# Seven split down products a slot, an input normalised a slot early, and routing tables in PSUM: one change to the front of a six-layer kernel

## The chip, the core and the metric

The kernel runs on one core of one Trainium2 chip. Its time is device microseconds of one execution. The engines of the core work in parallel, each through its own list of instructions in order, and they meet at semaphores: TensorE (PE, with its weight loads PEld), VectorE (DVE), ScalarE (ACT), GpSimd (POOL) and SyncE (SP), which here only starts transfers. Products are written by TensorE to PSUM, which has eight banks here: G, V, U, C, Y, Z and S0, S1.

## The reference, cut to what matters

Sixteen batches of 512 rows by 128 columns go through six layers, all in float32:

```
x = x + 0.5 * moe(layernorm(x))        # L0_ffn
x = x + gated_attention(layernorm(x))  # L0_attn
x = x + 0.5 * moe(layernorm(x))        # L0_ffn again, same weights
x = x + 0.5 * mlp(layernorm(x))        # L1_ffn, relu
x = x + softmax_attention(layernorm(x))  # L1_attn
x = x + 0.5 * mlp(layernorm(x))

moe(x): scores = sigmoid(x @ gate.T); the two best of 16, divided by (their sum + 1e-20) -> comb
        g = silu(x @ We_gate[e]); u = x @ We_up[e]          # 16 experts, 64 wide
        y = sum_e comb[e] * ((g * u) @ We_down[e])
        shared = (silu(x @ Ws_gate) * (x @ Ws_up)) @ Ws_down  # 128 wide
        return y + shared
```

The first four layers are the kernel's front (`build_front`), the last two its back. The change touches the front alone, and within it the MoE and its routing.

## The kernel before, in words

A batch lies on the chip as 128 partitions by T = 4 tiles by 128. The front works in slots. A slot computes one MoE layer of one batch, the main work, and beside it one other layer, the side work, of another batch. The loop `turns` (8) times `NM` (4) slots has side work ATT, MLP, ATT, MLP (`SIDE`); one slot without side work stands ahead of the loop and one behind it, 34 slots in all. The main input of a slot is prepared in the slot before it. The inputs are numbered q as the slots are; with odd q the input is a fresh batch in `xin`, loaded from memory; with even q it is the result `xw` of a side layer.

A slot has NT = 9 passes n = 0 to 8. Pass n takes 128 columns of the hidden width: n = 0 is the shared expert, n = 1 to 8 are two routed experts each. In each pass TensorE forms the gate product in G and the up product in U, each as three products of 512 columns of split operands (high times high, low times high, high times low; lines 903 to 905), and for n above 0 spreads the routing weights into C (line 955). ScalarE takes `s` = silu(G) (line 581). VectorE takes `su` = U*s (line 738) and `h` = C*su (line 749; for n = 0 `h` = U*s).

The down product of each `h` is made in one of two ways. In bank Y four products of 128x128 with float32 `h` as weights (`down`, line 910) give the result in its final layout. In bank V the result comes transposed: ScalarE rounds `h` to `hh` (`high`, line 565), GpSimd forms the rest `hl` = h - hh (`low`, line 432), and TensorE makes three products of 512 columns (lines 919, 921, 922), of which the first needs `hh` and the others stand behind a wait for `hl`. Before the change the passes 2 to 6 (V0 = 2, NV = 5) go to V and the passes 0, 1, 7 and 8 to Y; at the end ScalarE copies V to `vs` and TensorE adds its transposes to Y. I write V(k) or Y(k) for the down product of pass k. TensorE issues the down product of pass n-2 in pass n, except that Y(0) and Y(1) are issued a pass earlier, in passes 1 and 2.

The input's preparation runs through four engines: statistics on VectorE (`main_stats`), 1/sqrt and two 128x512 operations on GpSimd (`main_normalise`, result `z`), transposes of `z` into bank Z on TensorE (line 888), the rounding `xh` on ScalarE and its rest `xl` on VectorE (line 663), router products into Z (lines 895, 897), then the logits `lg`, an exponential on ScalarE and some 20 small VectorE operations on 128x64 tables (`routing_scores` to `routing_weights`, lines 675 to 724), and at last the transposes of `comb` into Z in the next slot's pass 0. The table `PREPARE` says in which pass each step stands in the lists.

The side work begins with statistics `mv_s` on VectorE, a scale and offset (`off_s`) on GpSimd, the normalised `zs` on ScalarE in pass 1, transposes into S0 by TensorE in pass 2 (line 963), `xhs` on ScalarE, `xls` on VectorE, and products of `xhs` and `xls`: those of the ATT slot at line 987, those of the MLP slot at lines 903 to 905 with output S.

No scheduler decides the order. Each engine's list is written out by hand in its own function `slot`, and GpSimd's in its loop; what stands earlier in a list is waited for by all that stands later.

Of the kernel before, what the change touches and what calls it, by code (L numbers as in the profile page):

```python
# [30 lines left out]
E = 16  # L31
# [3 lines left out]
V0, NV = 2, 5  # L35
# [22 lines left out]
class Chain:  # L58
# [114 lines left out]
def build_front(nc, weights, early, x_dram, mid_dram, ident_dram, staged_dram, tail_dram, turns):  # L173
    w = weights
    with ExitStack() as ctx:
# [34 lines left out]
        en = sb("en", [P, T, E])  # L210
        sc = sb("sc", [P, T, E])
        hit = sb("hit", [P, T, E])
        first = sb("first", [P, T, E])
        second = sb("second", [P, T, E])
        rest = sb("rest", [P, T, E])
        share = sb("share", [P, T, E])
        m1 = sb("m1", [P, T, 1])
        m2 = sb("m2", [P, T, 1])
        r1 = sb("r1", [P, T, 1])
        den = sb("den", [P, T, 1])  # L220
        comb = sb("comb", [P, T, E])
        comb2 = sb("comb2", [P, T, P])
        combh = sb("combh", [P, T, E], F32R)
# [33 lines left out]
        S = [ps(f"S{k}", [P, T, P]) for k in range(2)]  # L257

# [72 lines left out]
        block = ctx.enter_context(nc.Block())  # L331

# [66 lines left out]
        def _(pool):  # L399
# [20 lines left out]
            def main_normalise(q, i):  # L420
                rsqrt(rstd[:, :, 0], vpe, mv, mv_ready, mv_ready.at(i, q + 1), rstd_ready)
# [7 lines left out]
            def low(m, n, i):  # L429

                pool.wait_ge(hh_ready.sem, hh_ready.at(i, NV * m + n - V0 + 1))
                nc.gpsimd.tensor_tensor(hl[n % 3][:], h[n % 3][:], hh[n % 3][:],  # L432
                                        ALU.subtract).then_inc(hl_ready.sem, 1)
# [14 lines left out]
            own.step(nc.gpsimd.tensor_tensor(w["wdl"][:], w["wd"][:, V0:V0 + NV], w["wdh"][:], ALU.subtract))  # L448
            own.settle()
            main_normalise(0, 0)  # L450
            lows(-1, 0, range(V0, V0 + NV))
# [6 lines left out]
            for i in range(turns):  # L458
                for m in range(NM):
                    side_start(m, i, m)  # L460
                    if SIDE[m] == MLP:
                        main_normalise(m + 1, i)
                        lows(m, i, (2,))
                        side_bias(m, i, m)
                        lows(m, i, (3, 4, 5, 6))
                    else:
                        a = nth(m)
                        main_normalise(m + 1, i)
                        lows(m, i, (2,))
                        side_bias(m, i, m)  # L470
                        lows(m, i, (3,))
# [22 lines left out]
            lows(0, turns, (2, 3))  # L494
# [15 lines left out]
            lows(0, turns, (4, 5, 6))  # L510

        @block.scalar
        def _(act):
# [9 lines left out]
            def scores(q, i):  # L523
                act.wait_ge(lg_ready.sem, lg_ready.at(i, q + 1))
                nc.scalar.activation(en[:], lg[:], ACT.Exp, scale=-1.0).then_inc(score_ready.sem, 1)
# [37 lines left out]
            def high(m, n, i):  # L563
                act.wait_ge(h_ready.sem, h_ready.at(i, TE * m + n))
# [1443 lines left out]
```

## Time and profile before

| | |
|---|---|
| median of three runs | 1959.18 us (1956.84 to 1959.87) |
| the profiled execution | 1958.95 us, its span 1957.2 us |
| first slot's first gate product | 36.70 us |
| the last slot, from its first gate product to its last down product | 1094.86 to 1132.02 us |
| PE busy, share of the span | 1860.5 us, 95% |
| DVE, ACT, POOL busy | 1553.3, 1272.9, 886.6 us |
| granted TensorE clock, mean | 0.986 |

A busy share of TensorE counts modelled ends of products that overlap, so the distance between the starts of two products is the better measure of what one costs. A slot lasts about 32 us: ATT slots 32.3 us, MLP slots 31.8 us, measured between the first U products of one slot and of the next.

### The profile page before, as it was taken

Reading aid. Unit: us, or ns where it says so; the run is one execution under the profiler, and the core shown is the slowest. Engines: PE = TensorE matmul, PEld = TensorE weight load, DVE = VectorE, ACT = ScalarE, POOL = GpSimd, SP = SyncE. Lnnn points to the kernel's source line nnn. Section 1 sums busy time; section 2 is a strip of 40 time slices with the busy share of each in tenths; the row PEclk is TensorE's granted clock in tenths of the full one; section 3 lists DMA queues with packets and bytes.
Section 4 is the critical chain, followed back from the end, with each engine's and each line's share of the span. In section 5 each row is a group of like instructions: output and inputs, shape, how many; then the busy total and the mean of one; then the engine's idle time right before and its main releaser. Section 6 shows DMA issues by size and latency. Waiting matters only on the chain. (4 is left out here: it accounts for less than half of the span.)

```text
span 1957.2 us, 33103 instructions
## 1 busy us (share of the span) xinstructions
PE 1860.5 (95%) x11626; PEld 1258.0 (64%) x11626; DVE 1553.3 (79%) x3824; ACT 1272.9 (65%) x2383; POOL 886.6 (45%) x939
## 2 busy tenths in 40 slices
PE   2999999999999999999999889999999999999996
PEld 2788888888888888888888634444444444444433
DVE  5777777787777877787778479999999999999991
ACT  3555555555555565555555438888888888888884
POOL 2645654565556554655466323333333333333311
PEclk9999999999999999999999969999999999999998
DMA  3000000000000000000100032222222222222210
GB/s 134 7 12 1 12 12 12 1 12 12 12 1 12 12 12 12 1 12 12 37 2 6 6 96 90 90 91 91 91 91 91 89 88 88 88 92 84 92 39 12
DMA packets 49989, 85.74 MB, mean 44 GB/s; under 512 B 6752, under 2 KB 11104, under 8 KB 49760
## 3 DMA queue, kind: packets, MB, share of 16 engines
q1 hardware_dynamic: 47920, 81.85, 13.2%
q8 instruction: 93, 1.52, 0.3%
q10 hardware_dynamic: 1904, 1.78, 0.3%
q14 instruction: 72, 0.59, 0.1%
HBM read 49.26 MB, written 34.87 MB: 43 GB/s over the span
## 5 line engine op out<-in xcount | busy, mean ns | idle before, releaser
L1599 DVE TENSOR_REDUCE b_nm<-b_MX 128x1 f32<-128x512 f32 x1024 | 648.9, 683 | 46.5 <-PE b_MX L1707 30.0
L1491 ACT ACTIVATE b_pr<-b_ST 128x512 f32<-128x512 f32 x1024 | 550.1, 603 | 101.4 <-PE b_ST L1695 97.1
L581 ACT ACTIVATE s<-G 128x512 f32<-128x512 f32 x306 | 182.7, 597 | 184.5 <-PE G L905 158.5
L432 POOL TENSOR_TENSOR hl<-h,hh 128x512 fp32r<-128x512 f32 x170 | 219.3, 1290 | 180.6 <-ACT hh L565 180.6
L738 DVE TENSOR_TENSOR su<-U,s 128x512 f32<-128x512 f32 x272 | 187.2, 688 | 130.5 <-PE U L905 72.5
L1707 PE MATMUL b_MX<-b_kt,b_qt 32*128 32x512 f32 x768 | 240.8, 505 | 2.2 <-DVE b_nm L1599 1.8
L1695 PE MATMUL b_ST<-b_qt,b_kt 32*128 32x512 f32 x768 | 213.7, 494 | 6.1 <-ACT b_pr L1491 6.1
L1695 PEld LDWEIGHTS b_ST<-b_qt,b_kt 32*128 32x128 f32 x768 | 83.4, 181 | 204.0 <-ACT b_pr L1491 137.0
L749 DVE TENSOR_TENSOR h<-C,su 128x512 f32<-128x512 f32 x272 | 188.1, 691 | 9.3
L910 PE MATMUL Y<-w_wd,h 128*128 128x128 f32 x1088 | 145.3, 276 | 6.7 <-DVE h L749 6.7
L910 PEld LDWEIGHTS Y<-w_wd,h 128*128 128x128 f32 x1088 | 137.7, 192 | 16.8 <-DVE h L749 10.5
L1722 PE MATMUL b_PV<-b_pr,e_va 128*32 128x512 f32 x1024 | 139.0, 615 | 0.0
L903 PE MATMUL G<-xh,w_wgh 128*128 128x512 f32 x306 | 136.0, 444 | 0.7 <-ACT s L581 0.7
L1722 PE MATMUL b_PV<-b_pr,b_va 128*32 128x512 f32 x1024 | 136.4, 605 | 0.0
L903 PE MATMUL U<-xh,w_wuh 128*128 128x512 f32 x306 | 126.0, 412 | 1.1 <-DVE h L738 0.7
L905 PE MATMUL G<-xl,w_wgh 128*128 128x512 f32 x306 | 121.4, 397 | 0.0
L904 PE MATMUL G<-xh,w_wgl 128*128 128x512 f32 x306 | 121.2, 396 | 0.0
L905 PE MATMUL U<-xl,w_wuh 128*128 128x512 f32 x306 | 120.8, 395 | 0.0
L904 PE MATMUL U<-xh,w_wul 128*128 128x512 f32 x306 | 119.7, 391 | 0.0
L955 PE MATMUL C<-cT,w_pairs 128*128 128x512 f32 x272 | 107.7, 396 | 0.0
L1707 PEld LDWEIGHTS b_MX<-b_kt,b_qt 32*128 32x128 f32 x768 | 96.0, 185 | 15.8 <-DVE b_nm L1599 11.5
L565 ACT ACTIVATE hh<-h 128x512 fp32r<-128x512 f32 x170 | 105.9, 623 | 0.0
(308 smaller groups left out, 4075.4 us busy)
## 6 DMA issues: line engine op xcount, KB each, us to landing
b_kt<-staging SPq DMA_DIRECT2D x48, 256.0 KB, 3.0
b_qt<-staging SPq DMA_DIRECT2D x48, 256.0 KB, 3.4
staging<-e_khi SPq DMA_DIRECT2D x32, 256.0 KB, 2.9
staging<-e_qhi SPq DMA_DIRECT2D x32, 256.0 KB, 3.1
xin<-in_x SPq DMA_DIRECT2D x17, 256.0 KB, 2.8
mid<-xo SPq DMA_DIRECT2D x16, 256.0 KB, 2.0
staging<-e_klo SPq DMA_DIRECT2D x16, 256.0 KB, 3.0
staging<-e_qlo SPq DMA_DIRECT2D x16, 256.0 KB, 3.0
```

The lines of the kernel that those rows point to most:

```text
L432: nc.gpsimd.tensor_tensor(hl[n % 3][:], h[n % 3][:], hh[n % 3][:], ALU.subtract).then_inc(hl_ready.sem, 1)
L738: nc.vector.tensor_tensor(out[:], U[:], sbuf_s[n % 2][:], ALU.mult).then_inc(up_used.sem, 1)
L749: nc.vector.tensor_tensor(h[n % 3][:], C[:], su[n % 2][:], ALU.mult).then_inc(h_ready.sem, 1)
L903: pe.matmul(flat(bank), wh, flat(high), start=True, stop=False)
L904: pe.matmul(flat(bank), wl, flat(high), start=False, stop=False)
L905: return pe.matmul(flat(bank), wh, flat(low), start=False, stop=True)
L910: mm = pe.matmul(bank[:, t], hid[:, t], wd, start=(first and t == 0), stop=True, skip_group_check=True)
L1491: nc.scalar.activation(pr[k % 2][:, j], bank[:].rearrange("p a b -> p (a b)"), ACT.Exp, scale=SM_SCALE).then_inc(used["st"].sem, 1)
L1599: nc.vector.tensor_reduce(nm[g % 2][:, c:c + 1], bank[:].rearrange("p a b -> p (a b)"), AX.X, ALU.max).then_inc(used["mx"].sem, 1)
L1695: pe.matmul(flat(bank_of(B, "st", 0, u)), kt_[g][rows_of(j), k % T], flat(qt[g])[rows_of(j)], start=True, stop=True).then_inc(made["st"].s ...
L1707: pe.matmul(flat(bank_of(B, "mx", rel, u)), qt[g][rows_of(j), u // HG % T], flat(kt_[g])[rows_of(j)], start=True, stop=True).then_inc(made ...
L1722: mm = pe.matmul(flat(PV)[rows_of(j)], values_of(va[B.parity], kt, g, j), pr[k % 2][:, j], start=(k % (PAIR * T) == 0), stop=((k + 1) % (P ...
```

## The change

It does five things to the front.

1. `V0` goes and NV is 7: the passes 0 to 6 go to V, and 7 and 8 to Y. V(k) is issued in pass k+2 for all k, so nothing of the down products stands in pass 1. ScalarE and GpSimd have two more pieces (`high`, `low`) a slot, for passes 0 and 1. In pass 2 ScalarE's rounding of h(1) stands behind `side_high`; GpSimd's `low` of 0 and 1 stand behind the side's scale and offset.
2. The inputs with odd q, which the MLP slots use, have their statistics (pass 5) and `main_normalise` a slot earlier: in an MLP slot GpSimd now normalises the input m+1 behind `low` 0 and 1, and the input m+2 behind `low` 4. The first slot does this too.
3. In an ATT slot the transposes of `z` stand in pass 1 (before 3) and the router products in pass 2 (before 4); the exponential stays in pass 5. ScalarE's `xh` now stands before `zs` there.
4. The tables `en`, `sc`, `hit`, `rest`, `second`, `share` and `comb` lie in bank Z in place of SBUF. `combh` is gone: the rounding is written straight into `comb2`, one small operation less a slot. The two best scores share a tile, and their sum is a reduction.
5. `routed` of pass n at n of 3 and above always waits for `hl` of pass n-3.

The GpSimd list at the start of an MLP slot, before (`off_s`: the side's offset; `vpe`, `rstd`, `z`: `main_normalise`; `hl`: one `low` each; `xb`: side bias):

```order
L418 TENSOR_SCALAR off_s<-off_s 128x4
L405 TENSOR_TENSOR vpe<-mv,w_eps 128x4
L407 TENSOR_TENSOR rstd<-vpe,w_minus_half 128x4
L424 TENSOR_TENSOR z<-xw,mv 128x512
L427 TENSOR_TENSOR z<-z,rstd 128x512
L432 TENSOR_TENSOR hl<-h,hh 128x512
L445 TENSOR_TENSOR xb<-xw,w_b2h 128x512
L432 TENSOR_TENSOR hl<-h,hh 128x512 x4
```

And the same place now:

```order
L418 TENSOR_SCALAR off_s<-off_s 128x4
L435 TENSOR_TENSOR hl<-h,hh 128x512 x2
L405 TENSOR_TENSOR vpe<-mv,w_eps 128x4
L407 TENSOR_TENSOR rstd<-vpe,w_minus_half 128x4
L427 TENSOR_TENSOR z<-xw,mv 128x512
L430 TENSOR_TENSOR z<-z,rstd 128x512
L435 TENSOR_TENSOR hl<-h,hh 128x512
L448 TENSOR_TENSOR xb<-xw,w_b2h 128x512
L435 TENSOR_TENSOR hl<-h,hh 128x512 x2
L405 TENSOR_TENSOR vpe<-mv,w_eps 128x4
L407 TENSOR_TENSOR rstd<-vpe,w_minus_half 128x4
L427 TENSOR_TENSOR z<-xin,mv 128x512
```

Two `hl` moved ahead of the first normalisation, and a second normalisation came in between the `hl` of passes 4 and 5.

TensorE's list in an MLP slot, end of pass 2, before (C: routing weights; S: transposes of `zs`; Y: down product of pass 1):

```order
L955 MATMUL C<-cT,w_pairs 128x512
L963 MATMUL S<-w_ident,zs 128x128 x4
L910 MATMUL Y<-w_wd,h 128x128 x4
L903 MATMUL G<-xh,w_wgh 128x512
L904 MATMUL G<-xh,w_wgl 128x512
```

And now:

```order
L968 MATMUL C<-cT,w_pairs 128x512
L934 MATMUL V<-hh,w_wdh 128x512
L936 MATMUL V<-hh,w_wdl 128x512
L937 MATMUL V<-hl,w_wdh 128x512
L976 MATMUL S<-w_ident,zs 128x128 x4
L919 MATMUL G<-xh,w_wgh 128x512
```

The down product of pass 0 came here, in V and ahead of the transposes; Y(1) left.

TensorE's list in an ATT slot, end of pass 1, before:

```order
L955 MATMUL C<-cT,w_pairs 128x512
L910 MATMUL Y<-w_wd,h 128x128 x4
L903 MATMUL G<-xh,w_wgh 128x512
L904 MATMUL G<-xh,w_wgl 128x512
L905 MATMUL G<-xl,w_wgh 128x512
```

And now:

```order
L968 MATMUL C<-cT,w_pairs 128x512
L904 MATMUL Z<-w_ident,z 128x128 x4
L919 MATMUL G<-xh,w_wgh 128x512
L920 MATMUL G<-xh,w_wgl 128x512
L921 MATMUL G<-xl,w_wgh 128x512
```

The transposes of the next input took the place of Y(0).

The diff, cut to its core:

```diff
-V0, NV = 2, 5
+NV = 7
+INPUT_STATS = 5
 PREPARE = {
-    MLP: {"statistics": 1, "transpose": 4, "low": 4, "logits": 5, "scores": 6, "best": 6, "next": 7, "weights": 8},
-    ATT: {"statistics": 1, "transpose": 3, "low": 3, "logits": 4, "scores": 5, "best": 6, "next": 7, "weights": 8},
+    MLP: {"statistics": 1, "transpose": 4, "low": 4, "logits": 5, "exponential": 6, "scores": 6, "best": 6, "next": 7, "weights": 8},
+    ATT: {"transpose": 1, "low": 1, "logits": 2, "exponential": 5, "scores": 5, "best": 6, "next": 7, "weights": 8},
 }
...
+        en, sc, hit, rest, second, share = (Z[:, :, k * E:(k + 1) * E] for k in range(2, 8))
+        comb, total_score = en, second[:, :, 0:1]
...
             main_normalise(0, 0)
-            lows(-1, 0, range(V0, V0 + NV))
+            lows(-1, 0, range(5))
+            main_normalise(1, 0)
+            lows(-1, 0, range(5, NV))
...
                     if SIDE[m] == MLP:
+                        lows(m, i, (0, 1))
                         main_normalise(m + 1, i)
                         lows(m, i, (2,))
                         side_bias(m, i, m)
-                        lows(m, i, (3, 4, 5, 6))
+                        lows(m, i, (3, 4))
+                        if has_input(m + 2, i):
+                            main_normalise(m + 2, i)
+                        lows(m, i, (5, 6))
                     else:
                         a = nth(m)
-                        main_normalise(m + 1, i)
-                        lows(m, i, (2,))
+                        lows(m, i, (0, 1))
                         side_bias(m, i, m)
-                        lows(m, i, (3,))
+                        lows(m, i, (2, 3))
...
-                    if V0 < n <= V0 + NV:
+                    if 1 <= n <= NV and n != 2:
                         high(m, n - 1, i)
                     if n == 1 and side:
+                        if side == ATT:
+                            main_high(m + 1, i)
                         side_normalise(m, i, m)
                     if n == 2 and side:
                         side_high(i, m)
+                    if n == 2:
+                        high(m, n - 1, i)
...
-                step(nc.vector.tensor_copy(combh[:], comb[:]))
-                own.settle()
-                step(nc.vector.tensor_copy(comb2[:, :, 0:E], combh[:]))
+                step(nc.vector.tensor_copy(comb2[:, :, 0:E].bitcast(F32R), comb))
...
-                if n >= V0 + 3:
-                    dve.wait_ge(hl_ready.sem, hl_ready.at(i, NV * m + n - V0 - 2))
-                elif n >= 3:
-                    dve.wait_ge(down_done.sem, down_done.at(i, g0 + n - 2))
+                if n >= 3:
+                    dve.wait_ge(hl_ready.sem, hl_ready.at(i, NV * m + n - 2))
...
+                        if n == INPUT_STATS and side != ATT and has_input(m + 2, i):
+                            main_stats(m + 2, i)
...
-                    if n == 2 and side == MLP:
-                        side_transposes(i, m)
...
-                    if 1 <= n <= V0:
-                        moe_down(m, n - 1, i)
-                    if n >= V0 + 2:
+                    if n >= 2:
                         moe_down(m, n - 2, i)
                     if n == NT - 1:
                         moe_down(m, NT - 2, i)
+                    if n == 2 and side:
+                        side_transposes(i, m)
```

## Rows read from the trace of the kernel before

**Rows 1.** windows, a stretch of the front: engines busy, granted clock, DMA share, GB/s
```profile
480.00:600.00 120.00, 118.28 (x688) 100.98 (x687) 90.58 (x263) 65.53 (x118) 63.91 (x73) 1.00 0.03 10
```

**Rows 2.** timeline, TensorE (start, us, engine, line ...), MLP slot from 551.82
```profile
551.82 0.48 PE L903 MATMUL U<-xh,w_wuh 128*128 128x512 f32 x1
...
559.04 1.06 PE L910 MATMUL Y<-w_wd,h 128*128 128x128 f32 x8
559.85 0.48 PE L903 MATMUL G<-xh,w_wgh 128*128 128x512 f32 x1
...
565.22 0.40 PE L921 MATMUL V<-hh,w_wdl 128*128 128x512 f32 x1
...
565.68 0.40 PE L903 MATMUL G<-xh,w_wgh 128*128 128x512 f32 x1
```

**Rows 3.** timeline, GpSimd, the same MLP slot
```profile
556.51 0.23 POOL L418 TENSOR_SCALAR off_s<-off_s 128x4 f32<-128x4 f32 x1
558.54 0.20 POOL L405 TENSOR_TENSOR vpe<-mv,w_eps 128x4 f32<-128x4 f32 x1 [1.79 <-DVE mv L642]
...
562.06 1.30 POOL L432 TENSOR_TENSOR hl<-h,hh 128x512 fp32r<-128x512 f32 x1
```

**Rows 4.** timeline, ScalarE, the same MLP slot
```profile
559.24 0.60 ACT L543 ACTIVATE xhs<-S 128x512 fp32r<-128x512 f32 x1 [0.33 <-PE S L963]
```

**Rows 5.** timeline, TensorE, ATT slot from 519.49
```profile
519.49 0.48 PE L903 MATMUL U<-xh,w_wuh 128*128 128x512 f32 x1
...
528.66 0.45 PE L987 MATMUL S<-w_wkvuh,xhs 128*128 128x384 f32 x1
...
529.82 0.60 PE L888 MATMUL Z<-w_ident,z 128*128 128x128 f32 x4
530.17 0.48 PE L903 MATMUL G<-xh,w_wgh 128*128 128x512 f32 x1
...
532.92 0.18 PE L895 MATMUL Z<-w_router,xh 128*128 128x32 f32 x1
...
533.73 0.47 PE L919 MATMUL V<-hh,w_wdh 128*128 128x512 f32 x1
...
550.91 1.16 PE L910 MATMUL Y<-w_wd,h 128*128 128x128 f32 x8 [0.42 <-DVE h L749]
```

**Rows 6.** waits of weight loads from 120 to 960: total, times, longest, us
```profile
PEld S L1010 <- issue: 5.4, 13, 0.4
PEld S L987 <- DVE xls L762: 5.3, 13, 0.4
```

**Rows 7.** timeline, GpSimd, the ATT slot from 519.49
```profile
534.99 1.80 POOL L474 TENSOR_TENSOR kc<-kvu,w_sin_t 128x512 f32<-128x512 f32 x1 [1.35 <-ACT kvu L600]
...
546.38 1.30 POOL L432 TENSOR_TENSOR hl<-h,hh 128x512 fp32r<-128x512 f32 x1
548.03 1.28 POOL L490 TENSOR_TENSOR og<-on,uw 128x512 f32<-128x512 f32 x1 [0.36 <-ACT on L529]
```

**Rows 8.** timeline, VectorE, ATT and then MLP slot: one line, two lengths
```profile
548.30 1.09 DVE L710 TENSOR_TENSOR second<-hit,r 128x64 f32<-128x64 f32 x1
...
570.15 0.23 DVE L667 TENSOR_TENSOR lg<-Z,lb 128x64 f32<-128x64 f32 x1 [1.40 <-ACT lb L521]
...
579.08 0.22 DVE L710 TENSOR_TENSOR second<-hit,r 128x64 f32<-128x64 f32 x1
```

**Rows 9.** timeline, GpSimd, the first slot
```profile
50.11 0.20 POOL L405 TENSOR_TENSOR vpe<-mv,w_eps 128x4 f32<-128x4 f32 x1 [16.23 <-DVE mv L642]
...
53.61 2.55 POOL L432 TENSOR_TENSOR hl<-h,hh 128x512 fp32r<-128x512 f32 x2
```

**Rows 10.** timeline, TensorE, the first slot
```profile
55.65 0.39 PE L903 MATMUL G<-xh,w_wgh 128*128 128x512 f32 x1
```

**Rows 11.** timeline, ScalarE, the last slot
```profile
1107.21 0.63 ACT L565 ACTIVATE hh<-h 128x512 fp32r<-128x512 f32 x1
```

**Rows 12.** timeline, TensorE, the last slot
```profile
1115.69 1.11 PE L1024 MATMUL Z<-w_ident,e_xn 128*128 128x128 f32 x4 [7.96 <-POOL e_xn L509]
```

More of the change, by code:

```diff
@@ L209, in build_front @@
         lg = sb("lg", [P, T, E])
-        en = sb("en", [P, T, E])
-        sc = sb("sc", [P, T, E])
-        hit = sb("hit", [P, T, E])
         first = sb("first", [P, T, E])
[L214 to L218, printed above, removed]
+        best = sb("best", [P, T, 2])
+        m1, m2 = best[:, :, 0:1], best[:, :, 1:2]
         r1 = sb("r1", [P, T, 1])
         den = sb("den", [P, T, 1])
-        comb = sb("comb", [P, T, E])
         comb2 = sb("comb2", [P, T, P])
-        combh = sb("combh", [P, T, E], F32R)
         cT = [sb(f"cT{p}", [P, T, P], F32R) for p in range(2)]
@@ L509, in _ @@
             nc.gpsimd.tensor_tensor(early.xn[:], early.xn[:], w["lnsb"][:], ALU.add).then_inc(early.xn_ready.sem, 1)
-            lows(0, turns, (4, 5, 6))
+            lows(0, turns, range(4, NV))
         @block.scalar
@@ L593, in slot @@
                         side_high(i, m)
-                    if prepare and n == steps["logits"] + 1:
+                    if n == 2:
+                        high(m, n - 1, i)
+                    if prepare and n == steps["exponential"]:
                         scores(m + 1, i)
@@ L608, in slot @@
                     if prepare:
-                        if n == steps["transpose"]:
+                        if n == steps["transpose"] and side != ATT:
                             main_high(m + 1, i)
@@ L687, in routing_best @@
                 own.settle()
-                step(nc.vector.tensor_reduce(r1[:], hit[:], AX.X, ALU.max))
+                step(nc.vector.tensor_reduce(r1[:], hit, AX.X, ALU.max))
                 own.settle()
-                step(nc.vector.tensor_tensor(first[:], hit[:], wide(r1), ALU.is_equal))
+                step(nc.vector.tensor_tensor(first[:], hit, wide(r1[:]), ALU.is_equal))
                 own.settle()
-                step(nc.vector.scalar_tensor_tensor(out=rest[:], in0=first[:], scalar=-2.0, in1=sc[:],
+                step(nc.vector.scalar_tensor_tensor(out=rest, in0=first[:], scalar=-2.0, in1=sc,
@@ L693, in routing_best @@
                                                     op0=ALU.mult, op1=ALU.add))
                 own.settle()
-                step(nc.vector.tensor_reduce(m2[:], rest[:], AX.X, ALU.max))
+                step(nc.vector.tensor_reduce(m2, rest, AX.X, ALU.max))
             def routing_next(q, i):
                 own.settle()
-                step(nc.vector.tensor_tensor(hit[:], rest[:], wide(m2), ALU.is_equal))
-                step(nc.vector.tensor_tensor(den[:], m1[:], m2[:], ALU.add))
+                step(nc.vector.tensor_tensor(hit, rest, wide(m2), ALU.is_equal))
@@ L707, in routing_next @@
                 own.settle(1)
-                step(nc.vector.reciprocal(den[:], den[:]))
-                own.settle(1)
-                step(nc.vector.tensor_tensor(second[:], hit[:], wide(r1), ALU.is_equal))
-                own.settle(1)
-                step(nc.vector.tensor_tensor(share[:], sc[:], wide(den), ALU.mult))
+                step(nc.vector.reciprocal(den[:], total_score))
+                own.settle()
+                step(nc.vector.tensor_tensor(second, hit, wide(r1[:]), ALU.is_equal))
@@ L714, in routing_weights @@
+                step(nc.vector.tensor_tensor(share, sc, wide(den[:]), ALU.mult))
             def routing_weights(q, i):
                 own.settle(1)
-                step(nc.vector.tensor_tensor(first[:], first[:], second[:], ALU.add))
+                step(nc.vector.tensor_tensor(first[:], second, first[:], ALU.add))
                 own.settle()
-                step(nc.vector.tensor_tensor(comb[:], first[:], share[:], ALU.mult))
+                step(nc.vector.tensor_tensor(comb, share, first[:], ALU.mult))
@@ L847, in slot @@
                     if prepare:
-                        if n == steps["statistics"]:
+                        if n == steps.get("statistics"):
                             main_stats(m + 1, i)
```

71 lines of the change are left out of this document (38 added, 33 removed).

## The prediction, made before the change was run

> **What bounds the kernel now.** I read the share of busy time first, then stretches of the front, then TensorE's timeline through one MLP slot and one ATT slot with the others' beside it, then its waits. In a stretch of 120 us of the front TensorE is busy 118.28 us at full granted clock, the next engine 90.58 us [rows 1]: products stand one behind the other. So what the change removes from TensorE's list comes back in time, as long as what is queued behind waits does not rise. The back, whose code is untouched, I take as unchanged but for its start.
>
> Inside a slot TensorE has little slack against the chain of the side work: off_s, zs, the transposes, xhs, xls. In the MLP slot that starts at 551.82 the offset is made at 556.74, or 4.92 into the slot, and xhs starts at 7.42 [rows 3, 4]. In the ATT slot from 519.49 the products of xhs start at 9.17 [rows 5] and had to wait for xls in 13 of 13 slots of the window, 0.41 us each [rows 6]. These dates hang on the residual at the slot's start and on GpSimd, not on TensorE's content. The dates below that no row has are counted from there and are estimates: on TensorE 0.23 us a product of 512 columns, 0.35 four transposes, 0.81 a Y product or a group of router products, and 0.09 at the change back to long products [rows 2, 5]; on ScalarE and GpSimd the lengths of [rows 3, 4, 11].
>
> **The products removed and added, every slot.** A down product in Y costs 0.81 us (559.04 to 559.85), and the first product behind such small ones lasts 0.08 longer than the usual 0.40 [rows 2], so up to 0.09. One in V is three products of 0.23, as 565.22 to 565.68 shows for two [rows 2]: 0.69. Two a slot change: 1.62 to 1.80 go, 1.39 come, a gain of 0.2 to 0.4. Over 34 slots 8 to 14 us, if nothing waited.
>
> **The MLP slot: GpSimd's list.** Before, main_normalise(m+1) starts at 558.54 and ends at 562.06, 3.52 us, or 10.24 into the slot [rows 3]. The transposes of z wanted it at about 12.7, so it was hidden. Now `low` of passes 0 and 1 stands ahead. Low(0) runs from 4.9 to 6.2. V(0) is due at about 5.8, its second product at 6.0, so it waits 0.2. Low(1) needs hh(1), and that now stands behind xhs on ScalarE: xhs ends at 559.84, 8.02 into the slot [rows 4]; a rounding takes 0.63 [rows 11], the two overlap by 0.1, so hh(1) is there at 8.55. Low(1), 1.30 long [rows 3], ends at 9.86. The normalisation then ends at 13.4. TensorE, which in its own content arrives at 12.9, waits 0.5. Behind the normalisation stands low(2), 1.26 from start to the next start, done at 14.65, and V(2)'s second product waits for it. The last two products of V(2) take 0.46, so G of pass 5 starts at 15.15. Before it started at 565.68, 13.86 into the slot [rows 2]. **That is +1.3 a slot**, and includes the gain on the products, which is swallowed. Nothing brings it back: TensorE had no stall left in the rest of that slot. ScalarE, VectorE and the logits simply follow TensorE by 1.3.
>
> The second normalisation, of input m+2, stands behind low(4) and ahead of low(5). Its statistics follow the logits, end at about 21.2, GpSimd ends it at 24.8 and low(5) at 26.1; V(5)'s second product is due at 26.6. It costs nothing, with 0.5 us to spare; VectorE's 1.4 us for the statistics fall into a wait for U.
>
> Bounds for the MLP slot: 0.9, if hh(1) and the pieces run as tightly as overlaps allow and V(2) needs no restart; 1.8, if the shared-port waits of GpSimd, like the 1.80 us of L474 against 1.28 for a product of the same size [rows 7], strike once. I take 1.3.
>
> **The ATT slot.** Until the products of xhs at 9.17 nothing is gained or lost: TensorE loses Y(0) and Y(1), gets the transposes of z, the router and V(0), and still waits for the chain above (xl at about 5.4 holds the router by 0.4; the zs wait goes). Behind 9.17 the list loses the transposes (529.82 to 530.17, 0.35), the router (532.92 to 533.73, 0.81) [rows 5] and two slow starts of 0.09, and gets V(1), 0.69: -0.65. Waits that go: that before the attention product L1010, 5.4 us in 13 slots, of which I count half, 0.2 each [rows 6]; and that of the last down product, 0.42 behind h [rows 5] and 0.1 of restart. Waits that come: 0.2 at the query product, for the third bias; and more at V(6). GpSimd's run from L474 to low(6) is one chain; it starts with the silu of the keys, 0.1 later than 534.99 [rows 7] by my dates, and ends at about 28.0 into the slot. TensorE comes 0.7 earlier than before and waits 0.3 more there. Sum: -0.65 - 0.2 - 0.52 + 0.2 + 0.3 = **-0.87, say -0.85**. Bounds: -1.65 (all waits gone), -0.3 (GpSimd's chain holds the end).
>
> The wait for the last h goes for this reason. VectorE's L710 takes 1.09 us in the ATT slot and 0.22 in the MLP slot [rows 8]; the long one ends where GpSimd's product at 548.03, 1.28 long [rows 7], ends. So this small operation was held for GpSimd's whole operation. Both its inputs lay in SBUF; now one is in PSUM. The Trainium skill (SBUF — State Buffer, "SBUF: two separate sides") says that a VectorE operation with two SBUF inputs and a GpSimd operation that reads SBUF exclude each other for the whole instruction; by that rule, with which the trace agrees (1.09 against 0.22), the tables in Z end these waits. Against it: the skill (VectorE: DVE Perf Modes, "The TRN2 errata") gives a PSUM source 120 cycles where an SBUF source has 58, which by its clock would add an estimated 0.065 us to each of about 20 operations, 1.3 us a slot. The row of L667, which reads Z, has 0.23 against 0.22 for L710 from SBUF [rows 8], so the trace does not show it. What a write to PSUM costs VectorE no row shows. I bound it by nothing from below and by 0.22 (an operation twice as long) from above, and take nothing, as L667 is the nearest row; slack behind it in the routing steps is small in ATT slots, so at the upper end it would cost up to 1 us a slot.
>
> **The first slot.** `low` now stands behind the normalisation of input 0 while V(0) comes in pass 2. That normalisation starts at 50.11, and `hl` behind it at 53.61, two in 2.55 us [rows 9]; hl(0) lands at 54.9. TensorE reaches V(0) at 49.7 and stands until 54.97. From there three passes and more of its content lead to G of pass 5 at 60.5, before 55.65 [rows 10]: +4.85. Passes there are short, so V(5) in pass 7 (due at 67.8) waits for low(5) behind the second normalisation, done at 69.9; of this 2 us some 0.75 replaces a wait that was there, for ScalarE's table loads. **+5.6**, once. Bounds +4.5 and +7.5: after an idle time of 7.96 us the four transposes of 1115.69 take 1.11 us where 529.82 has 0.60 [rows 12, 5], so a long idle can be followed by slow products.
>
> **The last slot.** The back starts from the first attention input, whose normalisation on GpSimd stands behind low(3); TensorE waits 7.96 us for it [rows 12]. Low(3) needs hh(3), at 1107.21 before [rows 11]. With Y(0) out of pass 1 and V(0) for Y(1) h(3) comes 0.9 to 1 earlier. **-1.0**, bounds -1.8 and 0.
>
> **Sum.** 16 x 1.3 = +20.8; 16 x -0.85 = -13.6; +5.6; -1.0: +11.8. Against the profiled execution's 1958.95 (span 1957.2 and 1.75 around it) that gives 1970.75; the median of the runs, 1959.18, lies 0.2 above the profiled one. I predict 1971.
>
> **The rivals.** A. *The products' gain comes through* (faster). If hh(1) were early enough or the transposes of z had more slack, MLP slots would give -0.4 and ATT slots -0.85: 16 x -1.25 = -20, with 5.6 and -1 for the ends 1943.5. For it: TensorE has been the bound all along [rows 1]. Against: GpSimd's list holds 1.3 us of `low` twice ahead of 3.52, with 2.5 us of slack. It decides from hh(1) at 7.2 or earlier; xhs alone ends at 8.02.
> B. *Balance*: MLP slots at +0.9 and ATT slots at -1.3: -6.4 + 4.6, 1957. For it, ATT bounds are wide and all shared-port waits go.
> C. *The second normalisation binds too* (slower than forecast): V(5) waits in MLP slots. It has 0.5 us to spare; if statistics or GpSimd run 1.5 us later, +16: 1987.
> D. *PSUM tables are slow*: 0.5 us more in each ATT slot, +8: 1979. By the skill's PSUM figure (VectorE: DVE Perf Modes) it would be of about this size; no row here bears it out.
>
> **How the numbers follow.** Forecast 0.5, A 0.1, B 0.15, C 0.1, D 0.15. A difference of less than 0.2% (4 us) is about what cannot be told from none. Faster by that: A and a third of B, 0.14. Same: the rest of B and a little of the forecast's lower end, 0.13. Slower 0.73. The forecast's own spread is 1963 to 1979; with B and D whole, and C's nearer part, the range is 1955 to 1983.
>
> **What would show it.** In the changed profile: in each MLP slot an idle of about 0.5 us before the transposes of z, released by POOL z, and one of about 0.5 at the second product of V(2), released by POOL hl; MLP slots of 33.1 us, ATT slots of 31.5; L710's successor at 0.22 in all slots; one wait of about 5 us for hl in the first slot; the back's first product 10 to 13 us later. I am wrong if TensorE's stretches of the front still show no wait for POOL, or if ATT slots are not shorter.

## The result and the profile after

The changed kernel takes 1979.84 us (median of four runs, 1978.12 to 1980.72), the kernel before 1959.45 in the same comparison (1956.84 to 1959.87). The ratio is 1.0109, 95% interval 1.0094 to 1.0124: slower by 20 us. The profiled execution of the changed kernel took 1978.12 us, its span 1976.0, against 1958.95 and 1957.2 before; the mean granted clock is 0.984 against 0.986.

All slots of a kind are alike, so I measure a slot from one start of the `comb` transposes to the next. 16 slots of each kind lie between the first and the last of these.

| us | ATT slot | MLP slot | first slot |
|---|---|---|---|
| before | 32.33 | 31.82 | 27.51 |
| after | 31.61 | 33.25 | 35.85 |

16 x 1.43 - 16 x 0.72 + 8.34 = 19.7, and the span grew by 18.8. From the start to the first `comb` transposes it was 43.60 before and 42.96 after, but over all kernels below that stretch ranged from 41.99 to 45.42 in the profiled runs, whether or not its code was changed. So single times differ by 1 or 2 us for that alone, and the lengths of the ATT and MLP slots are the sharper measure: in either kernel all 16 of a kind lie within 0.1 us of each other. The first slot stands alone and is less sharp, as the experiments show.

TensorE in a stretch of the front, which answers to [rows 1] (busy us of PE, PEld, DVE, ACT, POOL, each with its count; granted clock; DMA share; GB/s):

```profile
480.00:600.00 120.00, 117.78 (x651) 96.80 (x650) 85.06 (x263) 68.81 (x122) 75.57 (x79) 1.00 0.02 5
```

GpSimd's work rose from 63.91 to 75.57 us there, VectorE's fell from 90.58 to 85.06. TensorE is idle for 0.5 us more and has fewer products in the same time. Its waits at weight loads between 120 and 960, which answer to [rows 6] (us in total, times, longest):

```profile
PEld V L936 <- POOL hl L435: 22.9, 39, 0.7
PEld Z L904 <- POOL z L430: 9.9, 13, 0.8
PEld U L919 <- DVE su L754: 8.3, 25, 0.5
PEld S L919 <- DVE kvu L816: 6.4, 13, 0.5
```

The two largest name GpSimd, and neither was there before in this size (`hl` stood at 2.8 us in 13 waits). In the MLP slot whose first U product starts at 563.82 they are here on TensorE, against [rows 2]:

```profile
577.32 0.66 PE L904 MATMUL Z<-w_ident,z 128*128 128x128 f32 x4 [0.32 <-POOL z L430]
577.73 0.48 PE L934 MATMUL V<-hh,w_wdh 128*128 128x512 f32 x1
578.55 0.50 PE L936 MATMUL V<-hh,w_wdl 128*128 128x512 f32 x1 [0.34 <-POOL hl L435]
578.89 0.39 PE L937 MATMUL V<-hl,w_wdh 128*128 128x512 f32 x1
579.12 0.39 PE L919 MATMUL G<-xh,w_wgh 128*128 128x512 f32 x1
```

And here on GpSimd, against [rows 3]; the second row shows it idle for 2.46 us until ScalarE has rounded h(1):

```profile
568.70 1.29 POOL L435 TENSOR_TENSOR hl<-h,hh 128x512 fp32r<-128x512 f32 x1
572.45 1.29 POOL L435 TENSOR_TENSOR hl<-h,hh 128x512 fp32r<-128x512 f32 x1 [2.46 <-ACT hh L576]
...
576.22 1.04 POOL L430 TENSOR_TENSOR z<-z,rstd 128x512 f32<-128x512 f32 x1
577.22 1.28 POOL L435 TENSOR_TENSOR hl<-h,hh 128x512 fp32r<-128x512 f32 x1
```

On ScalarE that rounding now stands right behind xhs, the operation of [rows 4]:

```profile
571.25 0.60 ACT L551 ACTIVATE xhs<-S 128x512 fp32r<-128x512 f32 x1 [0.35 <-PE S L976]
571.75 0.63 ACT L576 ACTIVATE hh<-h 128x512 fp32r<-128x512 f32 x1
```

In the ATT slot whose first U product starts at 532.22 the wait of the last Y products of [rows 5] is gone, and a short one stands at V(6):

```profile
544.85 0.34 PE L1000 MATMUL S<-w_wkvuh,xhs 128*128 128x384 f32 x1
...
560.41 0.50 PE L936 MATMUL V<-hh,w_wdl 128*128 128x512 f32 x1 [0.20 <-POOL hl L435]
...
563.01 1.06 PE L926 MATMUL Y<-w_wd,h 128*128 128x128 f32 x8
```

VectorE's operation that took 1.09 us in the ATT slot [rows 8] now reads and writes Z, and takes 0.23:

```profile
559.96 0.23 DVE L728 TENSOR_TENSOR Z<-Z,r 128x64 f32<-128x64 f32 x1
```

The first slot holds the wait that was forecast, and behind it something that was not in the sum. Products of 512 columns start 0.43 us apart, not 0.23:

```profile
48.66 0.40 PE L934 MATMUL V<-hh,w_wdh 128*128 128x512 f32 x1
54.31 0.80 PE L936 MATMUL V<-hh,w_wdl 128*128 128x512 f32 x1 [5.25 <-POOL hl L435]
54.90 0.63 PE L937 MATMUL V<-hl,w_wdh 128*128 128x512 f32 x1
55.33 0.63 PE L919 MATMUL G<-xh,w_wgh 128*128 128x512 f32 x1
...
70.75 0.50 PE L936 MATMUL V<-hh,w_wdl 128*128 128x512 f32 x1 [1.79 <-POOL hl L435]
```

The windows of that slot show the clock (the last columns as above). It reads 0.98 over the idle stretch and 0.50, the 1.2 GHz level, for 3.1 us once work is there again; and again for 3.0 us soon after the idle of 1.79:

```profile
48.50:54.30 5.80, 0.55 (x3) 0.12 (x1) 2.05 (x10) 0.56 (x2) 4.56 (x6) 0.98 0.00 0
54.30:57.40 3.10, 3.09 (x7) 2.49 (x8) 0.00 (x0) 0.55 (x2) 1.19 (x1) 0.50 0.00 0
57.40:60.00 2.60, 2.60 (x12) 2.10 (x11) 1.38 (x2) 1.02 (x3) 1.29 (x1) 0.98 0.00 0
...
71.40:74.40 3.00, 3.00 (x8) 2.31 (x7) 2.01 (x11) 0.60 (x1) 2.11 (x4) 0.50 0.00 0
```

About seven products in each stretch start 0.20 us later than they could: 2 x 1.4 = 2.8 us, an estimate from these rows.

In the last slot the back's first transposes came 0.25 us earlier than before, counted from the slot's `comb` transposes (1134.70 - 1116.93 = 17.77, before 1115.69 - 1097.67 = 18.02), with a wait like that of [rows 12]:

```profile
1134.70 1.11 PE L1037 MATMUL Z<-w_ident,e_xn 128*128 128x128 f32 x4 [8.07 <-POOL e_xn L517]
```

### The profile page after: what moved, and what is told of

It is laid out like the page before. It is cut to its first block and busy times, and to the rows that moved or that the text cites. A ratio compares the mean times of both kernels' runs of the same rounds, so it can differ in the third digit from the quotient of the medians.

```text
span 1976.0 us, 32590 instructions
## 1 busy us (share of the span) xinstructions
PE 1868.9 (95%) x11286; PEld 1228.8 (62%) x11286; DVE 1516.1 (77%) x3790; ACT 1306.8 (66%) x2451; POOL 971.5 (49%) x1007
## 5 line engine op out<-in xcount | busy, mean ns | idle before, releaser
L435 POOL TENSOR_TENSOR hl<-h,hh 128x512 fp32r<-128x512 f32 x238 | 307.4, 1292 | 136.8 <-ACT hh L576 136.8
L576 ACT ACTIVATE hh<-h 128x512 fp32r<-128x512 f32 x238 | 148.9, 625 | 0.1
L936 PE MATMUL V<-hh,w_wdl 128*128 128x512 f32 x238 | 100.1, 421 | 16.4 <-POOL hl L435 15.7
```

## The experiments

Each kernel was timed in five rounds against the kernel before, which had medians of 1958.1 to 1958.7 us. The slots are from the profiles, in us.

| kernel | median us | ratio, 95% interval | ATT | MLP | first |
|---|---|---|---|---|---|
| first_order | 1969.95 | 1.0050 [1.0038, 1.0063] | 31.61 | 33.25 | 28.63 |
| hh1_first | 1964.07 | 1.0023 [1.0014, 1.0033] | 31.60 | 32.33 | 36.60 |
| both_orders | 1957.03 | 0.9988 [0.9979, 0.9997] | 31.60 | 32.34 | 28.64 |
| second_last | 1978.72 | 1.0099 [1.0086, 1.0113] | 31.62 | 33.25 | 35.89 |
| tables_sbuf | 2001.87 | 1.0216 [1.0202, 1.0230] | 32.60 | 33.63 | 38.51 |
| tables_z_only | 1943.61 | 0.9924 [0.9911, 0.9937] | 31.40 | 31.86 | 28.16 |
| mixed | 1947.17 | 0.9942 [0.9928, 0.9955] | 31.60 | 31.85 | 27.44 |
| early_only | 1943.58 | 0.9924 [0.9911, 0.9936] | 31.30 | 31.86 | 27.95 |
| tables_ub | 1943.85 | 0.9922 [0.9909, 0.9934] | 31.40 | 31.86 | 27.69 |
| mixed_ub | 1940.17 | 0.9907 [0.9894, 0.9921] | 31.18 | 31.85 | 28.15 |
| late_y1 | 1942.68 | 0.9915 [0.9901, 0.9928] | 31.35 | 31.85 | 27.26 |
| early_ub | 1936.13 | 0.9884 [0.9869, 0.9899] | 30.88 | 31.85 | 27.43 |

The last column has a spread of its own. The changed kernel, second_last and hh1_first have the same lists in the first slot and took 35.85, 35.89 and 36.60 us there; mixed, early_only, mixed_ub, late_y1 and early_ub, which are also alike there, took 27.26 to 28.15. In hh1_first the products behind the first wait for `hl` stay 0.43 us apart for 4.3 us, in the changed kernel for 2.6.

**The orders.** first_order changes GpSimd's list in the first slot, in two places at once:

```diff
-            main_normalise(0, 0)
-            lows(-1, 0, range(5))
+            lows(-1, 0, range(2))
+            main_normalise(0, 0)
+            lows(-1, 0, range(2, NV))
             main_normalise(1, 0)
-            lows(-1, 0, range(5, NV))
```

> Only GpSimd's list of the first slot differs from the changed kernel: low 0 and 1 ahead of the normalisation of input 0, and the normalisation of input 1 behind low 6. My theory: the two waits of TensorE for hl there (5.25 and 1.79 us) and the slow products after each of them (about 1.3 and 1.4 us more than at full clock) are all of the first slot's +8.3 us, so the time falls by 8 to 9 us, to about 1971.3, and the products of passes 3 and 8 of that slot start 0.23 us apart, not 0.43. Rival: the slow products have nothing to do with the idle time and stay; then it falls by 6 to 7 us only. All other slots stay at 31.6 and 33.25 us.

The first slot gave 7.22 us back and no other slot moved; the median fell by 9.9. What is left of waits for GpSimd in that slot is 0.52 and 0.34 us, and this stretch, in which TensorE stood and then ran slowly in the changed kernel, is full, so the slow products went with the idle time:

```profile
50.50:56.00 5.50, 5.50 (x25) 4.32 (x23) 3.90 (x14) 2.89 (x6) 3.85 (x5) 1.00 0.00 0
```

hh1_first lets ScalarE round h(1) ahead of xhs in MLP slots:

```diff
+                    if n == 2 and side != ATT:
+                        high(m, n - 1, i)
                     if n == 2 and side:
                         side_high(i, m)
-                    if n == 2:
+                    if n == 2 and side == ATT:
                         high(m, n - 1, i)
```

ATT slots keep their order, and in the first slot, which has no `side_high`, nothing moves.

> In MLP slots ScalarE rounds h(1) ahead of xhs; nothing else differs from the changed kernel. My theory: the MLP slot is held by the chain xhs, hh(1), low(1), normalisation, low(2), V(2). hh(1) then ends at 7.6 us into the slot in place of 8.56, low(1) at 8.95, z is there at 12.5 and hl(2) at 13.8; G of pass 5 starts at about 14.4 in place of 15.3, an MLP slot lasts 32.4 in place of 33.27, and the time falls by 14 us to about 1965.5. Rival 1: the stall is there because TensorE's products in V cost more than those in Y; then no change. Rival 2: xhs later by 0.15 us delays xls and the hidden product, and the slot gains nothing.

The MLP slot fell by 0.92 us and the median by 15.8. In the changed kernel `low` of pass 1 starts 8.63 into the slot; that 2.46 us idle of GpSimd is now 1.50. Of the excess of 1.43 us a slot nearly two thirds was ScalarE's order alone. The rows say where the rest, 0.48 us against mixed below, lies. Counted from the `comb` transposes, the transposes of z start at 12.22, now without a wait, and in mixed at 11.94; G of pass 5 starts at 13.57 and 13.08. So 0.28 is lost ahead of z and 0.21 at V(2), whose second product still starts 0.43 us behind the first (0.32 in mixed).

both_orders has both edits.

> The changed kernel with both orders mended: ScalarE rounds h(1) ahead of xhs in MLP slots, and in the first slot GpSimd's pieces 0 and 1 stand ahead of the normalisation. Each alone took MLP slots from 33.25 to 32.34 and the first slot from 35.85 to 28.63. Theory (the two are independent): 1979.8 - 14.6 - 7.2 = 1958, no difference to the kernel before: what the tables gave is then spent on the rest of the MLP slots (16 x 0.5) and on the ATT slots. Rival (they share a wait): 1962 or more.

The effects add: 32.34 and 28.64 again, and 1957.03 us. With its faults of order mended, the change is where the kernel before was.

second_last moves GpSimd's second normalisation:

```diff
-                        if has_input(m + 2, i):
-                            main_normalise(m + 2, i)
                         lows(m, i, (5, 6))
+                        if has_input(m + 2, i):
+                            main_normalise(m + 2, i)
```

> The changed kernel with GpSimd's second normalisation of an MLP slot (input m+2) behind the hl of pass 6 in place of ahead of the hl of pass 5. Forecast's view (it is hidden): 1979, no change, MLP slots 33.25. Rival C (it holds V(5) back): MLP slots 0.3 or more shorter, 1974 or less.

No slot moved. Rival C is out: the work was hidden, as the sum had it.

**The tables.** tables_sbuf is the changed kernel with its tables in SBUF, tables_z_only the kernel before with the routing part of the change alone (with `combh` gone and the sum as a reduction). The edit of tables_sbuf:

```diff
-        en, sc, hit, rest, second, share = (Z[:, :, k * E:(k + 1) * E] for k in range(2, 8))
+        en, sc, hit, rest, second, share = (sb(f"tab{k}", [P, T, E])[:, :, :] for k in range(2, 8))
```

> The changed kernel with its routing tables in SBUF and not in bank Z. My theory: VectorE's small operations with two SBUF inputs wait again for GpSimd's operations, 1 to 1.3 us in pass 7 of an ATT slot, of which 0.84 is hidden behind the wait for silu: ATT slots 0.1 to 0.3 us longer, 2 to 5 us in all, 1982 to 1985. Rival: the tables' place does nothing for the time, 1979.8. Second rival: PSUM tables cost time, and it gets faster by up to 8 us.

> The kernel before with the routing part of the change alone: tables in bank Z, combh gone, sum of the two scores by a reduction. My theory: the 1.09 us of the operation that waits for GpSimd becomes 0.22, so h of pass 8 in ATT slots comes earlier and TensorE's wait for it (0.5 us with its restart) goes, and with it the 0.18 before the attention product: ATT slots 0.5 to 0.7 us shorter, 8 to 11 us in all, 1949 to 1951. Rival: the wait is taken over by the next one in line (silu of pass 8), and it gains under 3 us.

Both were under-estimated, the first by far: 22 us where 2 to 5 were expected, and 15 where 8 to 11 were. Grouped by line, VectorE in the kernel before between 120 and 960 (count, busy us, mean ns):

```profile
L699 DVE TENSOR_TENSOR hit<-rest,m 128x64 f32<-128x64 f32 x26 | 19.9, 765 | 0.0
L710 DVE TENSOR_TENSOR second<-hit,r 128x64 f32<-128x64 f32 x26 | 17.1, 657 | 0.0
L675 DVE TENSOR_SCALAR en<-en 128x64 f32<-128x64 f32 x27 | 9.2, 343 | 15.2 <-ACT en L525 15.2
L682 DVE TENSOR_TENSOR hit<-sc,m 128x64 f32<-128x64 f32 x26 | 8.1, 313 | 0.9
```

In the changed kernel the same four:

```profile
L728 DVE TENSOR_TENSOR Z<-Z,r 128x64 f32<-128x64 f32 x26 | 6.1, 233 | 0.9
L693 DVE TENSOR_SCALAR Z<-Z 128x64 f32<-128x64 f32 x26 | 6.1, 233 | 13.8 <-ACT Z L533 13.8
L700 DVE TENSOR_TENSOR Z<-Z,best 128x64 f32<-128x64 f32 x26 | 6.0, 232 | 0.9
...
L717 DVE TENSOR_TENSOR Z<-Z,best 128x64 f32<-128x64 f32 x26 | 5.8, 222 | 0.0
```

The prediction read one of the four, L710. L675 and L682 stand ahead of VectorE's `kvm`. The weight loads' wait for it went whole, but the first attention product came only 0.15 us earlier, 20.64 us behind the `comb` transposes and not 20.79, so counting half of that wait was right. The size that was too small is the one at the slot's end. In the kernel before, the last Y products follow at 550.91 [rows 5] behind this row:

```profile
549.89 0.60 PE L937 MATMUL Y<-w_ident,vs 128*128 128x128 f32 x4
```

In tables_z_only the same two stand closer:

```profile
545.46 0.60 PE L931 MATMUL Y<-w_ident,vs 128*128 128x128 f32 x4
545.89 1.06 PE L904 MATMUL Y<-w_wd,h 128*128 128x128 f32 x8
```

1.02 us from start to start became 0.43, and the next product, which came 0.91 behind the last Y products, comes 0.81 behind: 0.69 us, where 0.52 was forecast. The 0.42 in the bracket of [rows 5] counts from the modelled end of the operation before, so it is smaller than the delay. The other 0.24 of the 0.93 had come by V(6).

And tables_sbuf shows a cost in MLP slots that the kernel before did not have: the second normalisation puts GpSimd's operations beside the routing steps there. In the MLP slot whose `comb` transposes start at 577.27 each slow operation of VectorE ends where a `hl` of GpSimd ends:

```profile
601.29 1.33 POOL L435 TENSOR_TENSOR hl<-h,hh 128x512 fp32r<-128x512 f32 x1
601.51 1.19 DVE L704 TENSOR_TENSOR tab<-tab,w_ramp 128x64 f32<-128x64 f32 x1
...
603.23 1.29 POOL L435 TENSOR_TENSOR hl<-h,hh 128x512 fp32r<-128x512 f32 x1 [0.60 <-ACT hh L576]
603.25 1.35 DVE L710 SCALAR_TENSOR_TENSOR tab<-first,tab 128x64 f32<-128x64 f32 x1
```

The last MLP slot bears this out: it has no input m+2 and so no second normalisation, and took 33.26 us where the other 15 took 33.62 to 33.66. Without the tables in Z the early input would have cost 0.38 us in each MLP slot of the changed kernel. So the tables gave 0.93 a slot in the ATT slots of the kernel before, and in the changed one 0.99 and 0.38.

**Which passes go where.** mixed keeps the change, but in MLP slots and the first one the passes 0 and 1 go to Y again, ahead of the split ones; early_only does so in every slot. Three things go with it: the pieces `high` and `low` of these passes are gone, in MLP slots the transposes of `zs` stand ahead of the down product again, and in the first slot GpSimd's second normalisation stands behind all `low`. The edit's core (DIRECT is 2):

```diff
+def split_from(m):
+    return DIRECT if m < 0 or SIDE[m] == MLP else 0      # early_only: return DIRECT
...
-                if n < NV:
+                if split_from(m) <= n < NV:
...
+                    if 1 <= n <= split_from(m):
+                        moe_down(m, n - 1, i)
-                    if n >= 2:
+                    if n >= 2 + split_from(m):
                         moe_down(m, n - 2, i)
```

> The changed kernel, but in the MLP slots and in the first slot the down products of passes 0 and 1 go to Y again, so GpSimd's two pieces ahead of the normalisation are gone there; ATT slots keep all seven in V, the early input and the tables in Z stay. Theory (the MLP slots lose only by GpSimd's list ahead of the first normalisation): MLP slots return from 33.25 to 31.85 us, ATT slots stay at 31.6, the first slot about 28.5; 1959 - 16 x 0.73 gives 1947. Rival 1 (the second normalisation and its statistics cost something by themselves): MLP slots at 32.3, 1954. Rival 2 (the ATT slots lose in the changed kernel by what the MLP slot before them hands on late): ATT slots below 31.3, 1942.

> The same with the down products of passes 0 and 1 in Y in every slot: of the change only the early input and the tables in Z are left. The tables alone gave ATT slots of 31.40 us and MLP slots of 31.85. Theory GpSimd (in an ATT slot the chain from the silu of the keys over kc, qc, qc, hl, uw, ub, hl, off to the hl of pass 6 sets the end, and TensorE's list is no longer what ends last there): the waits that the early input takes from TensorE, 0.33 for zs and 0.3 for xls, bring nothing, the chain starts 0.2 later since Y(0), Y(1) and the router stand ahead of it: ATT 31.5 to 31.6, 1946. Theory TensorE (its list is the bound): ATT 30.8, 1934.

In mixed the MLP slot is back at 31.85 to the hundredth, so all of its loss came with V(0) and V(1) and the order that belongs to them, and the early input costs it nothing. In early_only the ATT slot is 31.30. So the two products in V make the ATT slot longer, by 0.30 us, though they are cheaper on TensorE by 0.12 each or more. The wait at V(6) is in early_only as it is in the changed kernel, 13 times in 13 slots, and this is the wait that theory GpSimd asked for. It expected 31.5 to 31.6, though; the chain's start was mis-sized.

**What ends last in an ATT slot.** early_ub and mixed_ub move one GpSimd product behind the last `low`:

```diff
-                        own.step(nc.gpsimd.tensor_tensor(ub[:], kvu[:, :, 2 * D:], w["lnb"][:], ALU.mult))
                         lows(m, i, (5,))
                         scale_offset(rstd2, off2, vpe2, mv2, mv2_ready, mv2_ready.at(i, a + 1), rstd2_ready)
                         lows(m, i, (6,))
+                        own.step(nc.gpsimd.tensor_tensor(ub[:], kvu[:, :, 2 * D:], w["lnb"][:], ALU.mult))
```

> As the one before, and in the ATT slots GpSimd's product ub (kvu times w_lnb, 1.26 us) stands behind the hl of pass 6 in place of ahead of the hl of pass 5, so that hl of pass 6 comes 1.26 us earlier and og some 0.9 later. Theory GpSimd: ATT slots fall by 0.6 to 0.7 to about 30.9, 1936. Theory TensorE: no difference to the kernel before it, or a loss by og, which the next slot's first transposes of S want; its slack is 0.8.

> The kernel with V in ATT slots and Y in MLP slots, with ub behind the hl of pass 6 as well. Theory GpSimd: the wait of 0.2 at V(6) and its slow start of 0.1 go, and what TensorE lost at the attention products: ATT slots 31.2, 1941; fewer products than with Y everywhere, but the products of keys and values start 0.25 later behind V(1). Theory TensorE: 30.6, 1931.

> The kernel before with the tables in Z, and ub behind the hl of pass 6. Theory: GpSimd's offset then waits for the statistics of the attention, the hl of pass 6 comes only 0.1 earlier, and TensorE's list with its waits for zs and xls (0.33 and 0.3) is as long as before: ATT slots 31.4, 1943.5; so the early input is worth 0.5 a slot, but only with ub out of the way. Rival (ub alone is the gain, the early input is worth nothing): ATT slots 30.9, 1936.

Both first ones fell by 0.42 us a slot, and tables_ub by nothing. In early_ub GpSimd now waits 0.80 us for the statistics of the attention, so of the 1.25 that left its list ahead of `low` of pass 6 only part came through:

```profile
530.26 1.27 POOL L449 TENSOR_TENSOR hl<-h,hh 128x512 fp32r<-128x512 f32 x1
532.33 0.20 POOL L426 TENSOR_TENSOR vpe<-mv,w_eps 128x4 f32<-128x4 f32 x1 [0.80 <-DVE mv L668]
...
534.21 1.29 POOL L449 TENSOR_TENSOR hl<-h,hh 128x512 fp32r<-128x512 f32 x1
535.46 1.29 POOL L506 TENSOR_TENSOR ub<-kvu,w_lnb 128x512 f32<-128x512 f32 x1
```

So the early input is worth 0.52 us a slot (31.40 against 30.88), but only with `ub` out of the way, and `ub` is worth nothing by itself. Two limits stood side by side, and either edit alone met the other: in tables_ub GpSimd waits 1.31 us for the same statistics, so `low` of pass 6 ends where it did. The rows of all kernels with tables in Z agree that this `low` dates the slot's end. Counted from the `comb` transposes it ends at 27.16 in tables_z_only, 27.05 in early_only, 27.36 in the changed kernel and 26.64 in early_ub, and the slot is 4.24 or 4.25 us longer in each. early_ub is the fastest kernel of this study, 1936.13 us, 1.2% below the kernel before. (Three of its four runs took 1934.28 to 1936.44; the fourth read 5818.69, which no other run came near and which I can't explain.)

**Place or kind.** late_y1 is early_ub with Y(1) in the ATT slots where V(1) stands in the changed kernel:

```diff
-                    if 1 <= n <= split_from(m):
+                    if 1 <= n <= split_from(m) and not (side == ATT and n == 2):
                         moe_down(m, n - 1, i)
+                    if side == ATT and n == 3:
+                        moe_down(m, 1, i)
```

> The fastest kernel so far (early input, tables in Z, passes 0 and 1 in Y, ub behind the hl of pass 6; ATT slots 30.88, MLP slots 31.85) with Y(1) in ATT slots a pass later, behind the first products of keys and values, where V(1) stands in the changed kernel. Theory place (the down product of pass 1 costs only because it moved out of the stretch in which TensorE waits for xhs and xls into the one behind it): these first products come 0.4 earlier, the second ones 0.5 later than with Y(1) in pass 2, ATT slots at 31.4, so 1944.5. Theory kind (V costs more than Y by what it asks of ScalarE and GpSimd): no change, 1936.

31.35 us: the place explains it. The first products of keys and values come 8.37 us behind the `comb` transposes, and 8.84 in early_ub, but the second ones at 12.03 against 11.57. With the pass-1 product in that place, Y for both passes costs more than V for both (31.35 against 31.18 in mixed_ub). V is the cheaper kind, as the forecast's rows said, by 0.17 us for the two; the place costs 0.47. (The 0.17 is not quite the kind alone, since the product of pass 0 stands in pass 1 as Y and in pass 2 as V.)

## Why the prediction came out right

The time was forecast at 1971, 9 us low, within the range and on the right side. The range was 28 us wide, so what counts is the mechanism. By its steps:

- **The MLP slot** (forecast +1.3, measured +1.43). Every date held: h(1) rounded by 8.55 us into the slot (measured 572.38 - 563.82 = 8.56), z done at 13.4 (13.44), V(2) let go at 14.65 (14.73), G of pass 5 at 15.15 (15.30). The two waits of 0.5 us that were forecast are there too, if read from start to start: the transposes of z begin 0.72 us behind the product ahead of them (576.60 to 577.32) where 0.23 is usual, and V(2)'s second product 0.82 behind its first where it was 0.32. The 0.32 and 0.34 in the rows' brackets count from modelled ends. The missing 0.13 is the start behind a wait: z's transposes and V(2)'s second product are followed 0.41 and 0.34 us later by the next product, not 0.35 and 0.23. hh1_first and mixed show the cause by experiment.
- **The ATT slot** (forecast -0.85, measured -0.72). The sum was close, its parts were not. Tables: -0.72 in the forecast (0.52 for the last h, 0.2 at the attention products), -0.93 measured (0.69 for the last h and 0.24 ahead of it). The early input and V(0), V(1): -0.13 in the forecast, measured +0.2 (31.40 to 31.61), which is -0.10 and +0.30. The two errors nearly cancelled, and that is luck. The step that failed is "it starts with the silu of the keys, 0.1 later": with V(1) between the two groups of products of keys and values, the second group starts 11.85 us behind the `comb` transposes (544.85 - 533.00) against 11.60 with the tables alone (527.68 - 516.08). GpSimd's chain to `low` of pass 6 begins 0.24 later than with the tables alone, that `low` ends 0.20 later, and V(6) comes with it.
- **The first slot** (forecast +5.6, measured +8.34). The two waits were as forecast, 5.25 and 1.79 us. What was mis-sized is the speed behind them: the slow products were kept as an upper end, +7.5, and not put into the sum. They cost 2.8 us, and 5.6 + 2.8 = 8.4. That this fits so well is partly luck. The terms that the prediction writes out, 4.85 + 2 - 0.75, come to 6.1 and not to 5.6, and first slots with the same lists differ by up to 0.9 us. The smaller number was the nearer one, because before the change two starts in that place were late, by 0.9 and 0.5 us, and not one:

```profile
63.27 0.40 PE L922 MATMUL V<-hl,w_wdh 128*128 128x512 f32 x1
64.40 0.50 PE L903 MATMUL G<-xh,w_wgh 128*128 128x512 f32 x1 [0.73 <-ACT s L581]
...
64.97 0.40 PE L905 MATMUL G<-xl,w_wgh 128*128 128x512 f32 x1
65.70 0.50 PE L903 MATMUL U<-xh,w_wuh 128*128 128x512 f32 x1 [0.34 <-DVE su L738]
```

The price of the slow products could have been read in the kernel before, on TensorE behind the wait for the first `comb`, where products also start 0.43 us apart:

```profile
43.60 1.09 PE L945 MATMUL Z<-w_ident,comb 128*128 128x128 f32 x4 [3.99 <-DVE comb L724]
...
44.91 0.63 PE L904 MATMUL G<-xh,w_wgl 128*128 128x512 f32 x1
45.34 0.63 PE L905 MATMUL G<-xl,w_wgh 128*128 128x512 f32 x1
```

- **The last slot** (forecast -1.0, measured -0.25). The step that failed is that h(3) comes 0.9 to 1 earlier: the prediction left V(1) out. h(3) gets rounded only behind ScalarE's silu of pass 4, and that stands behind V(1), a product that now lies in pass 3. Counted from the `comb` transposes the rounding of h(3) starts at 9.30 (1126.23 - 1116.93) against 9.54 before (1107.21 - 1097.67). The experiments bear it out: the back's first transposes start 17.74 to 17.78 us behind the `comb` ones in every kernel that has V(0) and V(1) in the last slot, and 18.02 or 18.03 in every one that has Y there, wherever the tables and the input are.
- **Hidden work.** The second normalisation was hidden: `low` of pass 5 ends at 589.91 and V(5)'s second product starts at 590.56, 0.65 us to spare where 0.5 was forecast, and second_last shows that the place costs nothing.

Sum of the corrections: 16 x 0.13 + 16 x 0.13 + 2.7 + 0.75 = 7.6. The profiled execution took 1978.12 us where the sum gave 1970.75, so 7.4 are to be explained.

Rival D, slow tables in PSUM, is out: the four operations above take 0.22 to 0.23 us in Z, and the reciprocal 0.566 against 0.553 (means of L695 and L677). Its time, 1979, is near the measured one by chance. Rival B, the balance, is out too: MLP slots lost 1.43 and not 0.9, and ATT slots gained 0.72 and not 1.3. Rival A, the products' gain, did not come in the slots that count: with passes 0 and 1 in V the MLP slot is longer by 0.48 us even with ScalarE's order mended (32.33 against 31.85), and the ATT slot by 0.30. Only the last slot kept 0.25 of it. What stays open is how the 0.28 us that the MLP slot loses ahead of z divides between the late products of V(0) and of xhs. Also, tables_z_only takes away one small operation and turns a sum into a reduction, which was not tried apart; tables_sbuf has both as well and is slow, so the place of the tables is what counts.

## What to carry to other kernels

In lists kept in order by hand, price a moved instruction by the stretch it leaves and the one it enters: a dearer product in a stretch that waits anyway beats a cheaper one behind the point where a chain starts. When an edit should save time and does not, look for a second limit that ends at nearly the same moment, and lift both before judging either. An aggregate of independent edits hides good ones: here 15 us of gain from the tables were inside a change that lost 20.

## What the runs showed of the hardware

- A small VectorE operation with its inputs in SBUF took up to 1.35 us in place of 0.2 while GpSimd worked, also when other GpSimd work was merely moved beside it (tables_sbuf, MLP slots; in the last of them, without that work, the 0.38 us are gone). With its tables in PSUM it took 0.22 to 0.23, writes to PSUM included, and this placement changed a kernel by 15 to 22 us in about 1950.
- Two idles of TensorE, 5.25 and 1.79 us long, were followed by 3.1 and 3.0 us at a granted clock of 0.50, the second after some 0.65 us at 0.82. The stretch of the idle itself read 0.98. Behind the first wait for `comb` (3.99 to 4.13 us) the same products start 0.43 us apart for 3 to 5 us too, but there the granted clock reads 1.00 in the kernels before and after, and 0.51 in hh1_first (44.50 to 50.60). So the distance between starts is the surer sign of slow products. How long they stay slow differs from run to run: behind the first wait for `hl`, with the same lists, 2.6 us in the changed kernel and 4.3 in hh1_first. The waits of 0.32 and 0.34 us in MLP slots left the clock at 1.00 over 120 us.
